# Attention step of an adaLN block on one Trainium2 core: the probabilities' transposes in two groups of eight

## What is computed

```python
h = layernorm(x) * (1 + ca) + sa
q, k, v = h @ Wq + bq, h @ Wk + bk, h @ Wv + bv       # W = codes * scales, 16 heads of 128
attn = softmax(q @ k.T / sqrt(128))                   # per batch and head, 512 x 512
x = x + ga * ((attn @ v) @ Wo + bo)
h = layernorm(x) * (1 + cb) + sb
x = x + gb * (h @ W.T + lora(top-2 of 8 experts, h))
```

## Time and profile before

| | us |
|---|---|
| median of 3 runs | 919.41 |
| lowest and highest | 918.55, 919.74 |
| span of the profiled execution | 918.8 |
| PE busy in it | 885.4 |
| DVE, ACT, POOL busy | 640.5, 553.9, 496.0 |
| first and last group of transposes, start | 35.73, 856.73 |

### The profile page before, as it was taken

One profiled execution on the slowest core, in us unless ns is written; L12 is line 12 of the kernel. 1 busy time (PEld: TensorE's weight loads), 2 busy tenths in 40 slices (PEclk: granted clock), 3 DMA queues, 4 the chain that ended last, 5 costly groups with the idle time before them and its releaser, 6 DMA issues.

```text
span 918.8 us, 15117 instructions
## 1 busy us (share of the span) xinstructions
PE 885.4 (96%) x4802; PEld 748.2 (81%) x4802; DVE 640.5 (70%) x1275; ACT 553.9 (60%) x1176; POOL 496.0 (54%) x497
## 2 busy tenths in 40 slices
PE   3899999999999999999999999999999999999878
PEld 2678888888888888888888888888888888887667
DVE  3678776776767666776767766677676767667884
ACT  2566766666666666666666666666666666665541
POOL 4554575457644575446654575546654575443341
PEclk9999999999999999999999999999999999999999
DMA  6200001000100011000100010000100001000002
GB/s 193 83 24 1 1 24 46 24 1 24 46 23 0 0 34 34 23 0 23 46 23 0 0 43 25 23 0 23 46 23 0 0 27 44 1 1 1 1 1 91
DMA packets 24657, 23.48 MB, mean 26 GB/s; under 512 B 3186, under 2 KB 24116, under 8 KB 24628
## 3 DMA queue, kind: packets, MB, share of 16 engines
q1 hardware_dynamic: 24628, 23.11, 8.1%
HBM read 21.01 MB, written 2.10 MB: 25 GB/s over the span
## 4 chain that ended last, share of the span: by engine, by line
PE 89%; DVE 5%; issue 1%; SPq 1%; ACT 1%; DMA 1%; POOL 0%; ACTq 0%; DVEq 0%; POOLq 0%
PE tr L1032 12%; PE qv L882 7%; PE qv L884 6%; PE qv L883 6%; PE score L882 6%; PE score L884 6%; PE score L883 6%; PE o L884 6%; PE o L882 6%; PE o L883 6%; PE ky L882 5%; PE ky L884 5%; PE ky L883 5%; PE y L882 2%; PE y L883 2%; PE y L884 2%
## 5 line engine op out<-in xcount | busy, mean ns | idle before, releaser
L348 POOL TENSOR_TENSOR prob<-prob,inv_sum 128x512 f32<-128x512 f32 x256 | 263.6, 1042 | 122.4 <-DVE inv_sum L720 122.4
L479 ACT ACTIVATE prob<-score,neg_max 128x512 f32<-128x512 f32 x256 | 176.4, 689 | 184.4 <-DVE neg_max L715 183.2
L715 DVE TENSOR_REDUCE neg_max<-score 128x1 f32<-128x512 f32 x256 | 177.0, 691 | 92.6 <-PE score L884 87.1
L724 DVE TENSOR_TENSOR pT_lo<-tr,pT_hi 128x512 fp32r<-128x512 f32 x256 | 174.7, 683 | 54.5 <-ACT pT_hi L493 54.4
L336 POOL TENSOR_TENSOR v_lo<-v,v_hi 128x512 fp32r<-128x512 f32 x64 | 82.6, 1291 | 237.2 <-ACT v L445 237.2
L493 ACT ACTIVATE pT_hi<-tr 128x512 fp32r<-128x512 f32 x256 | 152.2, 594 | 76.7 <-PE tr L1032 76.3
L1032 PE MATMUL tr<-ident,prob 128*128 128x128 f32 x1024 | 154.2, 273 | 2.6 <-DVE pT_lo L724 2.6
L1032 PEld LDWEIGHTS tr<-ident,prob 128*128 128x128 f32 x1024 | 124.4, 140 | 31.5 <-issue 4.2
L882 PE MATMUL score<-k_hi,q_hi 128*128 128x512 f32 x256 | 100.5, 392 | 1.3 <-ACT prob L479 1.3
L882 PE MATMUL o<-pT_hi,v_hi 128*128 128x512 f32 x256 | 99.8, 390 | 0.7 <-DVE pT_lo L724 0.7
L884 PE MATMUL o<-pT_hi,v_lo 128*128 128x512 f32 x256 | 100.1, 391 | 0.0
(11 more groups left out here) (227 smaller groups left out, 1805.8 us busy)
## 6 DMA issues: line engine op xcount, KB each, us to landing
stage<-in_L_attn_wq_codes_dram SPq DMA_DIRECT2D x8, 256.0 KB
stage<-in_L_attn_wq_scales_dram SPq DMA_DIRECT2D x16, 128.0 KB
stage<-in_L_attn_wk_codes_dram SPq DMA_DIRECT2D x8, 256.0 KB
stage<-in_L_attn_wk_scales_dram SPq DMA_DIRECT2D x16, 128.0 KB
stage<-in_L_attn_wv_codes_dram SPq DMA_DIRECT2D x8, 256.0 KB
stage<-in_L_attn_wv_scales_dram SPq DMA_DIRECT2D x16, 128.0 KB
stage<-in_L_attn_wo_codes_dram SPq DMA_DIRECT2D x8, 256.0 KB
stage<-in_L_attn_wo_scales_dram SPq DMA_DIRECT2D x16, 128.0 KB
```

What stands on the lines that cost most here:

```text
L348: pool.tensor_tensor(prob[:, i], prob[:, i], inv_sum[:, i:i + 1].to_broadcast([P, S]), ALU.mult).then_inc(prob_ok, 1)
L479: act.activation(prob[:, i], score_ps[i % 2][:, :], ACT.Exp, bias=neg_max[:, i:i + 1], accum_out=row_sum[:, i:i + 1]).then_inc(exp_ok, 1)
L715: dve.tensor_reduce(neg_max[:, i:i + 1], score_ps[i % 2][:, :], AX.X, ALU.max, negate=True).then_inc(max_ok, 1)
L724: dve.tensor_tensor(pT_lo[:, s % 2, :, i * P:(i + 1) * P], tr_ps[i % 2][:, :].rearrange("p (k q) -> p k q", k=QT), pT_hi[:, s % 2, :, i * ...
```

## The change

In each step PE transposes parts 0 and 1 one behind the other, ahead of the q projection, and parts 2 and 3 behind it, ahead of k. The banks are the same: `pT_bank` is tr0, tr1, tr0, tr1. ACT and DVE evacuate in the new order: parts 0 and 1, q, parts 2 and 3, k. For the first two groups of a step the wait on `p_ok` is left out, since the weighted sum ahead of them has waited for all four parts of the step before. In step 0 of a pair ACT's wait for `o_hi_ok` stands behind `prob_high(1)` instead of ahead of `prob_high(0)`. In step 63 the modulation rows stand behind part 1, and the modulation columns behind part 3. In steps 1 and 3 of the first pair DVE's `normalise` stands behind `prob_low(3)`. No instruction of the computation is added or removed.

```diff
+        pT_bank = [*tr_ps, *tr_ps]
...
-                    if s == 0 and not start:
-                        act.wait_ge(o_hi_ok, n)
                     prob_high(0)
-                    if end:
-                        act.wait_ge(mod2_mm, 2)
-                        act.activation(mod_row[:, S:2 * S], ky_ps[0:B, :], ACT.Copy).then_inc(mod2_ev, 1)
+                    prob_high(1)
                     if s == 0:
+                        if not start:
+                            act.wait_ge(o_hi_ok, n)
                         act.activation(bias_now[:, 2], bias[:, 2, bass.ds(2 * p, 2)], ACT.Copy).then_inc(bias_ok, 1)
                         act.wait_ge(bias_ok, 2 * p + 2)
                     if not end:
                         q_high(n + 2, (s + 1) % 2)
-                    prob_high(1)
+                    else:
+                        act.wait_ge(mod2_mm, 2)
+                        act.activation(mod_row[:, S:2 * S], ky_ps[0:B, :], ACT.Copy).then_inc(mod2_ev, 1)
+                    prob_high(2)
+                    prob_high(3)
                     if not end:
                         k_high(n + 2, (s + 1) % 2)
...
                     prob_low(0)
+                    prob_low(1)
                     if not end:
                         q_low(n + 2, head_slice(p, s + 1))
-                    prob_low(1)
+                    prob_low(2)
+                    prob_low(3)
                     if not end:
                         k_low(n + 2, head_slice(p, s + 1))
...
-                        if not (start and i < 2):
+                        if i >= 2:
                             pe.wait_ge(p_ok, QT * n + i - 1)
...
                     transpose_probs(0)
+                    transpose_probs(1)
                     if not end:
...
                         project(qv_ps, "q", nxt % 2, batch_of(nxt)).then_inc(q_mm, 1)
...
-                    transpose_probs(1)
+                    transpose_probs(2)
+                    transpose_probs(3)
                     if not end:
...
                         project(ky_ps, "k", nxt % 2, batch_of(nxt)).then_inc(k_mm, 1)
...
-                    transpose_probs(2)
...
-                    transpose_probs(3)
```

More of the change, by code:

```diff
@@ L493, in prob_high @@
                         act.activation(pT_hi[:, s % 2, :, i * P:(i + 1) * P],
-                                       tr_ps[i % 2][:, :].rearrange("p (k q) -> p k q", k=QT), ACT.Copy).then_inc(p_hi_ok, 1)
-                    if s == 0 and not start:
-                        act.wait_ge(o_hi_ok, n)
+                                       pT_bank[i][:, :].rearrange("p (k q) -> p k q", k=QT), ACT.Copy).then_inc(p_hi_ok, 1)
                     prob_high(0)
-                    if end:
-                        act.wait_ge(mod2_mm, 2)
-                        act.activation(mod_row[:, S:2 * S], ky_ps[0:B, :], ACT.Copy).then_inc(mod2_ev, 1)
+                    prob_high(1)
                     if s == 0:
+                        if not start:
+                            act.wait_ge(o_hi_ok, n)
                         act.activation(bias_now[:, 2], bias[:, 2, bass.ds(2 * p, 2)], ACT.Copy).then_inc(bias_ok, 1)
@@ L513, in pair @@
                             act.activation(modT[:, k:k + DC], mod_columns(qv_ps, i), ACT.Copy).then_inc(mod_ok, 1)
-                    prob_high(2)
-                    if end:
                         act.wait_ge(mod2_tr, 2)
                         act.activation(modT[:, CB:CB + DC], mod_columns(ky_ps, 0), ACT.Copy, bias=1.0).then_inc(mod_ok, 1)
-                    prob_high(3)
-                    if end:
                         act.wait_ge(ga_bo_ok, DC)
@@ L724, in prob_low @@
                         dve.tensor_tensor(pT_lo[:, s % 2, :, i * P:(i + 1) * P],
-                                          tr_ps[i % 2][:, :].rearrange("p (k q) -> p k q", k=QT),
+                                          pT_bank[i][:, :].rearrange("p (k q) -> p k q", k=QT),
                                           pT_hi[:, s % 2, :, i * P:(i + 1) * P].bitcast(f32), ALU.subtract).then_inc(p_ok, 1)
@@ L774, in pair @@
                             dve.tensor_scalar(ga_bo[:, c], modT[:, GA + c], bo_sb[:, c:c + 1], None, ALU.mult).then_inc(ga_bo_ok, 1)
-                    prob_low(2)
                     if new:
                         normalise(new)
-                    prob_low(3)
                     if not start and not end:
@@ L1028, in transpose_probs @@
                             pe.wait_ge(h_hi, DC * INPUT_AT[s - 1] + i + 1)
-                        if not (start and i < 2):
+                        if i >= 2:
                             pe.wait_ge(p_ok, QT * n + i - 1)
                         for kt in range(QT):
-                            ins = pe.transpose(tr_ps[i % 2][:, kt * P:(kt + 1) * P], prob[:, i, kt * P:(kt + 1) * P], ident[:, :])
+                            ins = pe.transpose(pT_bank[i][:, kt * P:(kt + 1) * P], prob[:, i, kt * P:(kt + 1) * P], ident[:, :])
                         ins.then_inc(p_tr, 1)
                     transpose_probs(0)
+                    transpose_probs(1)
                     if not end:
```

## The result

The changed kernel takes 986.63 us (median of 4 runs, 985.39 to 987.36), against 918.98 us for the kernel before in the same comparison (917.46 to 919.74): a ratio of 1.0732, 95% interval 1.0717 to 1.0748. It is 67.7 us slower. The forecast was 987.5 us.

The account below looks back on a forecast made before the run. TensorE's own queue was taken to bound the kernel. Terms 64.5 + 1.3 - 0.9 + 0.4 + 1.6 + 1.2 = 68.1 us, added to 919.4, gave 987.5 us, range 976 to 1000.

Parts of the forecast that it names:

- What bounds the kernel: Before the change TensorE's own queue sets the time, busy 96% of the span; ACT and DVE are late nowhere.
- When TensorE comes to group 2: Third of a step's four transpose groups, numbered 0 to 3: TensorE reaches it 2.27 us into the step.
- When group 2 may start: Third transpose group waits for pT_lo of part 0, done at 2.98; starts at 3.13, a stall of 0.86 us.
- the sum of +1.04: Whole loop step: with both stalls it lasts 13.84 us against 12.80 before.
- Steps that differ: Corrections within steps 1 to 62: late o_lo +1.3, step 0 of middle pairs -0.9, first pair +0.4 us.
- Step 0 of all and the end: Kernel's two ends: first step 1.6 us longer, last step and the way to the end 1.2 us longer.
- The turns saved: Two fewer turns from transposes to projections per step, 0.01 to 0.02 us each, winning nothing because a wait follows.
- What is queued behind the waits: k_lo visible at 7.39, needed at 7.69; POOL's four in a row delay group 1, the second transpose group, by 0.6 us.
- That the waits would be met: Rival at the third transpose group: pT_lo is out in time, only saved turns count, 917.4 us; chance 0.03.
- Only the first wait landing: Rival: part 1 follows part 0 early enough, each step is +0.89 us, time 978 us; chance 0.04.
- The clock: Rival: TensorE's stalls drop its clock to 1.2 GHz, some 1096 us if every step, 1042 if every second; chance 0.04.
- The second wait behind it: Rival: second out projection waits for k_lo, or reaction to p_ok is longer; 1000 us; chance 0.10.

Follow-up runs that it names:

- Experiment 2: Changed kernel with parts 2 and 3 transposed into the two score banks instead of reusing the transpose banks: 918.60 us, ratio 0.9992 to the kernel before.
- experiments 1: Changed kernel with both the q and k projections between the two groups of eight transposes: 917.98 us against 919.08 for the kernel before.
- experiment 4: Kernel before with only TensorE's order changed, ACT and DVE keeping their old order: 1061.78 us, ratio 1.1554.

## Why the prediction was right, point by point

- *What bounds the kernel*: right. The chain from the last maximum to `pT_lo` stands in the changed step where it stood, and TensorE now waits for its end.
- *When TensorE comes to group 2, 2.27 us into the step*: right. Experiment 2, which lets it go, starts it at 2.26.
- *When group 2 may start, 3.13, and group 3, 3.72*: 3.13 in the trace; the 0.20 us that the waiting group of eight is longer fits 0.13 for the second wait and 0.03 for each restart. Step by step the sum of +1.04 met 1.03.
- *Steps that differ.* Steps 1 to 62: 65.3 us were reckoned (64.5 + 1.3 - 0.9 + 0.4). From the first group of step 1 to that of step 63 the trace of before has 852.06 - 52.18 = 799.9 us, and the changed kernel's 65.7 more. Within them one term failed in sign: step 0 of a middle pair was to win 0.15 on top, since q_high no longer holds up v; it did not. There `pT_lo` of part 0 ends 3.17 us into the step, before as after, and not 2.98: the last exponential comes 0.08 later, and `o_lo` another 0.11, as in steps 1 and 2. The extra 0.16 us before were v's wait, but beside them stood this later chain, which I didn't read. It is now paid, and the step is 14.04 us long, 0.2 more than the others.
- *Step 0 of all and the end, 2.8 us*: mis-sized, 0.3 measured. Step 0 grew by 0.4, not 1.6. Up to its scores it did grow by 1.5: from the wait's end there are 47.34 - 41.92 = 5.42 us, against 45.58 - 41.65 = 3.93 before. But 1.1 of that came back, most of it since the kernel before had another wait right behind, which the prediction left out. Its timeline of PE:

```profile
45.58 0.48 PE L882 MATMUL score<-k_hi,q_hi 128*128 128x512 f32 x1
...
47.24 0.50 PE L882 MATMUL o<-pT_hi,v_hi 128*128 128x512 f32 x1 [0.72 <-DVE pT_lo L724]
```

In the changed kernel group 3 stands ahead of k and v, and that wait is gone. The stretch of halved clock came at 43.0 instead of 42.0, and lay on k and the start of v where it had lain on v. Step 63 and the rest of the way, in which before had a second such stretch (at 888.5) and the changed kernel none, got 0.4 shorter instead of 1.2 longer. The first transposes of all start 0.3 later; nothing ahead of them was changed.
- *The turns saved*: right in kind, and small as reckoned: 0.016 a turn, and 0.01 measured in experiments 1 and 2; and right that the change itself gets nothing of it. The Trainium skill's rule on rotating banks ("Perfetto Trace Analysis", Matmuls) didn't cover the evacuation here: the banks came free 2.98 and 3.57 us into the step, and TensorE wanted them again at 2.27 and 2.71.
- *What is queued behind the waits*: k_lo was to be visible at 7.39 with 0.30 to spare. It ends at 549.90 + 0.75 = 550.65, 7.24 into the step, and no wait of PE for it shows. POOL's four in a row put group 1 off by 0.12 us and not 0.6 (0.56 into the step from 459.94, where others have 0.44), for POOL starts them earlier in the longer step.
- *Rivals.* That the waits would be met is ruled out by the trace. Only the first wait landing: both did. The clock: the changed kernel's is at the upper level but for 3.41 us from 43.0. The row PEclk alone wouldn't show such a stretch, since one of its digits stands for 24.6 us; the window in the last section does. The second wait behind it didn't come.
- *What the profile would show*: PE's idle time before the transposes is 50.4 us and its busy share 92%, where 60 and 90% were forecast. The stalls are as long as forecast; the profile hides part of each, as said above.
- *Span and time*: the span grew by 66.0, the median by 67.7. In the run that was profiled, 986.55 us, 1.8 us lie around the span; the 0.6 that I took for before compared a span with other executions' median. So the forecast of the time, 0.9 us off, is closer than its parts: the span was forecast 2.1 too long (986.9 against 984.8), and what lies around it 1.2 too short. That they cancel is luck; 62 equal steps, 64.5 of the 68.1 us, are not.

## What to carry to other kernels

A busy engine's order is free to change only within the slack of what it must wait for. Before two groups are drawn together, take the chain that frees the buffer from its last release by that engine (here the last scores) to its end, and compare it with what now stands between the two uses of the buffer; if it is longer, as here, the difference is paid in full in every turn of the loop. Keep the evacuations in the order in which the producer needs them back, and where the chain can't be shortened, a buffer that is idle just then (here the score banks) or a longer piece of work in between does the same. A handover from one engine to the next is to be measured where the receiver was idle: a row in which it was busy contains its queue.

## What the hardware showed beyond that

The granted clock in experiment 4. Windows of its trace, with its columns: us, busy time of PE, PEld, DVE, ACT and POOL, granted clock, DMA share and GB/s:

```profile
47.20:170.00 122.80, 104.70 (x554) 84.62 (x553) 81.16 (x164) 68.32 (x145) 61.37 (x60) 1.00 0.06 18
170.00:173.41 3.41, 3.35 (x10) 2.90 (x11) 0.00 (x0) 0.00 (x0) 0.00 (x0) 0.51 0.00 0
173.41:187.10 13.69, 11.96 (x66) 9.81 (x66) 8.97 (x17) 7.99 (x17) 6.83 (x7) 1.00 0.02 3
```

And one of the changed kernel's, for nearly all of its span:

```profile
46.50:984.00 937.50, 878.47 (x4689) 723.44 (x4687) 623.42 (x1222) 545.57 (x1141) 471.63 (x462) 1.00 0.06 18
```

With one wait of 0.7 and a short second one a step (PE listed as busy for 94% of the stretch), the clock stays at its upper level, 2.4 GHz. With two waits of 0.7 to 0.9 on both sides of four transposes (busy 85%), it went to 1.2 GHz for 3.41 us at 170.0, and at five more places in the middle of the kernel and one near its end. All six in the middle begin in a step 0 or 1 of a middle pair, behind the second wait (the first is 4.84 into the step from 165.21). There the two waits are among the longest, listed with 0.93 and 0.88 or 0.82 and 0.91, against 0.70 and 0.93 in most steps; but six of the twelve such steps passed without. A step with such a stretch lasts 1.5 to 1.7 us longer than its like without one (16.59 against 14.95), so they make some 10 of the 143 us that experiment 4 lost. So the rival of the falling clock did happen, but in experiment 4 and not in the change, whose four timed executions all have a granted clock of 0.998 (experiment 4's 0.981 to 0.989). The Trainium skill ("TensorE: Matmul & The Clock Gate", A second HAM failure mode) tells of brief idles between groups that make the clock swing; experiment 4's trace agrees, the changed kernel's, with one such idle a step, does not.
